# Attention without the turn of its result on TensorE, and values made for four key tiles at a time in place of two

## What is computed

```python
mod = (_silu(L0_c) @ L0_wmod).reshape(L0_c.shape[0], 6, 1, -1)
sa, ca, ga, sb, cb, gb = ...
h = _layernorm(x, axis=-1) * (1 + ca) + sa
x = x + ga * _L0_attn_ref(h, ...)        # q, k of 128 = 64 rope + 64 nope, latent of 32
h = _layernorm(x, axis=-1) * (1 + cb) + sb
x = x + gb * _L0_ffn_ref(h, ...)         # top 6 of 32 experts, plus the shared one

# inside _L0_attn_ref
scores = jnp.einsum('bhsd,bhtd->bhst', query, key) * scale
attn = jax.nn.softmax(scores.astype(jnp.float32), axis=-1)
out = jnp.einsum('bhst,bhtd->bhsd', attn, v)
return out.transpose(0, 2, 1, 3).reshape(B, S, H * VD) @ o_w.T
```

## Time and profile before

| | us |
|---|---|
| median of 3 runs | 2083.45 |
| range | 2078.28 to 2084.25 |
| the profiled execution | 2077.61 |
| its span, first to last instruction | 2075.7 |

### The profile page before, as it was taken

One profiled execution on the slowest core, in us unless ns is written; L12 is line 12 of the kernel. 1 busy time (PEld: TensorE's weight loads), 2 busy tenths in 40 slices (PEclk: granted clock), 3 DMA queues, 4 the chain that ended last, 5 costly groups with the idle time before them and its releaser, 6 DMA issues. The chain is left out here.

```text
span 2075.7 us, 44742 instructions
## 1 busy us (share of the span) xinstructions
PE 1918.5 (92%) x14050; PEld 1015.4 (49%) x14050; DVE 1354.4 (65%) x2858; ACT 1389.4 (67%) x1924; POOL 1347.8 (65%) x804
## 2 busy tenths in 40 slices
PE   8969999999999999999999999998855499999996
PEld 6623444444444444444444444443733367777765
DVE  5867777777777877777777778771532245555553
ACT  5617888888888888888888888887520135555543
POOL 2327888888888888888888888888256313333330
PEclk9969999999999999999999999999977699999998
DMA  6179970000000000000000000000123429999988
GB/s 235 46 311 406 407 274 0 0 0 0 0 0 0 0 0 0 0 0 0 0 0 0 0 0 0 0 1 3 55 81 123 140 94 338 343 347 346 337 277 288
DMA packets 87873, 231.12 MB, mean 111 GB/s; under 512 B 12048, under 2 KB 45072, under 8 KB 87696
## 3 DMA queue, kind: packets, MB, share of 16 engines
q1 hardware_dynamic: 77072, 200.32, 27.0%
q0 software_dynamic: 10752, 30.16, 3.8%
HBM read 126.33 MB, written 104.10 MB: 111 GB/s over the span
## 5 line engine op out<-in xcount | busy, mean ns | idle before, releaser
L813 POOL TENSOR_TENSOR prob_lo<-prob,prob_hi 128x1024 f16<-128x1024 f32 x512 | 1085.1, 2141 | 246.8 <-ACT prob_hi L836 246.8
L885 DVE TENSOR_REDUCE maxes<-ring 128x1 f32<-128x512 f32 x1024 | 645.0, 683 | 195.4 <-PE ring L987 187.6
L834 ACT ACTIVATE prob<-p_s,prob_scale 128x1024 f32<-128x1024 f32 x512 | 570.3, 1114 | 262.1 <-PE p_s L1021 260.6
L836 ACT ACTIVATE prob_hi<-p_s,prob_scale 128x1024 f16<-128x1024 f32 x512 | 570.2, 1114 | 0.0
L987 PE MATMUL ring<-kr_hi,qr_hi 64*128 64x512 f16 x1024 | 379.6, 385 | 13.6 <-DVE qc_hi L872 7.4
L987 PE MATMUL ring<-kc_pair,qc_hi 64*128 64x512 f16 x1024 | 375.5, 384 | 0.0
L1289 POOL DMA_INDIRECT ranked_out<-y,dest x128 | 122.7, 959 | 268.6 <-DVE y L1591 265.4
L1021 PE MATMUL p_s<-qr_lo,kr_hi 64*128 64x512 f16 x1024 | 293.0, 377 | 0.0
L1021 PE MATMUL p_s<-qr_hi,kr_lo 64*128 64x512 f16 x1024 | 283.2, 377 | 0.0
L1021 PE MATMUL p_s<-qr_hi,kr_hi 64*128 64x512 f16 x1024 | 250.3, 382 | 1.6 <-ACT prob_hi L836 1.5
L1021 PE MATMUL p_s<-qc_lo,kc_one 33*128 33x512 f16 x1024 | 248.1, 379 | 0.0
(11 more groups left out here) (253 smaller groups left out, 2665.9 us busy)
## 6 DMA issues: line engine op xcount, KB each, us to landing
w<-in_experts SPq DMA_DIRECT2D x128, 608.0 KB
expert_rows<-zeros SPq DMA_DIRECT2D x129, 544.0 KB, 7.7
rows<-expert_rows SPq DMA_DIRECT2D x128, 136.0 KB
got<-ranked_out SPq DMA_DIRECT2D x16, 768.0 KB, 10.4
wqb<-in_wqb SPq DMA_DIRECT2D x8, 768.0 KB, 5.0
cbar<-in_woT SPq DMA_DIRECT2D x1, 2048.0 KB, 16.3
ranked_out<-y,dest POOLq DMA_INDIRECT x128
out<-x SPq DMA_DIRECT2D x16, 128.0 KB, 3.6
```

Of the source, the lines that this page charges most:

```text
L813: gp.tensor_tensor(prob_lo[s % NB][:, :], prob[s % 2][:, :], prob_hi[s % NB][:, :], ALU.subtract).then_inc(lo_ready, 1)
L834: act.activation(prob[s % 2][:, :], p_s[s % 2][:, :], ACT.Exp, bias=prob_scale[:, :], scale=SCALE / W_SCALE)
L836: act.activation(prob_hi[s % NB][:, :], p_s[s % 2][:, :], ACT.Exp, bias=prob_scale[:, :], scale=SCALE / W_SCALE).then_inc(p_ready, 1)
L885: v.tensor_reduce(maxes[:, at:at + 1], bank[:, :], AX.X, ALU.max).then_inc(ring_used, 1)
```

## The change

Three things change.

- **No turn.** `turn` is gone from attention, and `turn_att` with its copies from `mixture`. `copy_out` writes one of two `att_t`. SyncE sends the two rows of sums to DRAM (`send_sums`) and fetches them back as 128 partitions of 8 (`fetch_sums`); VectorE inverts them (`invert`, at the start of group 1); SyncE sends the inverses to DRAM and spreads them over 32 partitions in each half (`send_recips`, `spread_recips`); VectorE multiplies `att_t` in place (`scale`, at the start of the last group); and SyncE stores the result in `cbar`, which now holds channels on partitions (`store_heads`). The last half-head's share of this is done at the head of `mixture`, where the projection of the second 1024 tokens waits for it.
- **`BATCH` = 4.** `plan` has four groups. Group `g` scores tiles `4g + 2` to `4g + 5` and then weighs tiles `4g` to `4g + 3`. The 32 maxima stand in groups 0 to 2 (10, 12 and 10), rope after the scores of group 2, rest after those of group 3, rows in group 3.
- **SyncE's order.** The blocks of `slots_dram` are cleared five at a time in the first 26 half-heads, each five between `spread_recips` and `store_heads`.

One wait is merged as well: the load of `wkz` counts on `ld_ov`.

```diff
-STEPS_V = 2 * 9
+STEPS_V = 2 * 8
...
-BATCH = 2
+BATCH = 4
+MOVES = 96
...
+def send_sums(sp, k, scaling, done):
+    att_t, recip_wide, sums, sums_dram, recips_dram = scaling
+    for c in range(2):
+        sp.dma_start(sums_dram[k:k + 1, c * QC:(c + 1) * QC],
+                     att_t[k % 2][c * CP + C:c * CP + C + 1, :]).then_inc(done, 16)
+def fetch_sums(sp, k, scaling, done):
+    sp.dma_start(sums[:, :], sums_dram[k:k + 1, :].rearrange("o (p j) -> (o p) j", p=P)).then_inc(done, 16)
+def send_recips(sp, k, scaling, done):
+    sp.dma_start(recips_dram[k:k + 1, :].rearrange("o (p j) -> (o p) j", p=P), sums[:, :]).then_inc(done, 16)
+def spread_recips(sp, k, scaling, done):
+    for c in range(2):
+        sp.dma_start(recip_wide[k % 2][c * CP:c * CP + C, :],
+                     recips_dram[k:k + 1, c * QC:(c + 1) * QC].to_broadcast([C, QC])).then_inc(done, 16)
...
-        MAX_AT = (MORE, LESS, MORE, MORE, LESS, MORE, NONE, NONE)
+        MAX_AT = (((0, 4, 7, 11, 16), (2, 5, 9, 13, 18)), ((0, 4, 7, 10, 14, 17), (2, 5, 9, 12, 15, 19)),
+                  ((1, 6, 10, 14, 17), (3, 8, 12, 15, 19)), ((), ()))
...
+            for k in range(2 * H - 1):
+                sp.wait_ge(o_copied, k + 2)
+                send_sums(sp, k, scaling, moved)
+                sp.wait_ge(moved, MOVES * k + 32)
+                fetch_sums(sp, k, scaling, moved)
+                if k:
+                    sp.wait_ge(stored, 32 * k)
+                    sp.sem_inc(freed, 1)
+                sp.wait_ge(answered, 2 * k + 1)
+                send_recips(sp, k, scaling, moved)
+                sp.wait_ge(moved, MOVES * k + 64)
+                spread_recips(sp, k, scaling, moved)
+                clear(min(5 * k, BLANKS), min(5 * k + 5, BLANKS))
+                sp.wait_ge(answered, 2 * k + 2)
+                store_heads(sp, k, scaling, cbar, stored)
...
-            def copy_out(m):
+            def copy_out(m, half):
                 v.wait_ge(o_mm, 16 * m + 16 + NB)
-                v.tensor_copy(att_t[:, :], p_o[:, :]).then_inc(o_copied, 1)
+                v.wait_ge(freed, m + 1)
+                v.tensor_copy(att_t[half][:, :], p_o[:, :]).then_inc(o_copied, 1)
+            def invert(m):
+                v.wait_ge(moved, MOVES * m + 48)
+                v.reciprocal(sums[:, :], sums[:, :]).then_inc(answered, 1)
+            def scale(m, half):
+                v.wait_ge(moved, MOVES * m + MOVES)
+                v.wait_ge(o_copied, m + 2)
+                v.tensor_tensor(att_t[half][0:CP + C, :], att_t[half][0:CP + C, :], recip_wide[half][0:CP + C, :],
+                                ALU.mult).then_inc(answered, 1)
...
                 for g in range(len(MAX_AT)):
-                    for now in plan(g, first, more, after):
+                    if g == 1 and not first:
+                        invert(m - 1)
+                    if g == len(MAX_AT) - 1 and not first:
+                        scale(m - 1, 1 - half)
+                    for now in plan(g, more, after):
...
-            def turn(m, use, bank):
-                pe.wait_ge(o_copied, m + 2)
-                pe.wait_ge(ring_used, use + 1)
-                for b in range(4):
-                    last = pe.transpose(bank[:, b * P:(b + 1) * P], att_t[:, b * P:(b + 1) * P], ident[:, :])
...
             def project(t):
-                pe.wait_ge(ct_ready, t + 1)
+                if t == T // 2:
+                    pe.wait_ge(stored, 64 * H)
```

165 lines of the change are left out of this document (86 added, 79 removed).

## The result

The changed kernel takes **2210.84 us** (median of 4 runs, 2204.77 to 2218.78) against 2082.75 for the kernel before, run beside it (4 runs, 2078.28 to 2084.25). The ratio is 1.0621 with a 95% interval of 1.0579 to 1.0663: **slower by 6.2%**. The forecast was 2190, with 2155 to 2225 for its unknown terms. The profiled execution is the slowest of the four, 2218.78 us with a span of 2216.8; against the profiled execution of before it is 141 us longer.

The account below looks back on a forecast made before the run. TensorE was taken as the bound, busy 40.00 of 40 us. Half-heads rise from 40.4 to 44.3 us, 122 us together; less 9 in `mixture`, net +113 on 2077.6 gives 2190 us, range 2155 to 2225.

Parts of the forecast that it names:

- The sign and the mechanism: Attention: slower, as TensorE idles for ScalarE's exponentials before scores, some 5 us in a half-head; net +113 us.
- The group's period: Each four-tile group in attention: 4.59 + 0.31 + 2.71 = 7.61 us, plus 0.216 per counted pair, plus any projection of 1.32.
- A and D: First and fourth of four tiles scored in a row; D may start 4.59 us after the start of A's last pair.
- The second wait: Start of a half-head: the fourth maximum waits for VectorE's split, copy and first reduction; 0.9 us, all on the path.
- The turn's 0.58 us: TensorE's turn, removed from each half-head of attention: a gain of 0.58 us.
- `scale` costs nothing: VectorE's multiply between rope work and `rows`, about the copy's 0.69 us; the delayed row has over 2 us to spare.
- The sum: 29 half-heads 113 us, the first 4.5, the 31st 2.5, the last 2: 122 more; less `mixture`'s 9, net +113.
- `mixture`: After attention: gives back 9 us, 2 for the last turn and 7 for turning back 16 tiles.
- The covered wait: Attention: other work covers the exponentials, leaving only gains; 57 us less, 2021 us, chance 0.07.
- The clock: Attention: TensorE's pauses drop its clock to 1.2 GHz for a quarter of the path; some 185 us more, 2375, chance 0.05.
- The DMAs: `invert` comes 5 us late in the 26 half-heads that also clear; 130 us more, 2320, chance 0.04.
- The smaller loss: Exponentials overlap more or the second wait is hidden; a half-head loses 2 to 3 us, 2130 to 2155, chance 0.05.

Follow-up runs that it names:

- experiment 2: The kernel before with groups of four tiles, the turn kept at the start of the second group; 2223.7 us, 1.068 of before.
- experiment 3: The changed kernel with each tile's first exponential on 512 of its 1024 columns; 2136.67 us, 1.0265 of before.
- experiment 5: The changed kernel with the one unused bank place moved from behind the first maximum to behind the sixth; 2195.95 us, 1.0572 of before.
- experiment 1: The changed kernel with groups of two tiles again and the old places of the maxima, still without the turn; 2078.31 us, 0.9988 of before.
- Experiment 7: The changed kernel with only group 0's maxima moved, so that its first tile's five pairs stand alone; 2157.88 us, 1.0377 of before.
- experiment 11: Two-tile groups, no turn, unused bank behind the sixth maximum, `scale` ahead of the fifth group's reductions on 8 of 512 columns; 2055.52 us, 0.9904 of before.
- 8: The changed kernel with all 32 maxima spread by another table over the first three groups; 2134.45 us, 1.0276 of before.
- experiment 4: The kernel before with each tile's first exponential on 512 of its 1024 columns; 2072.61 us, 0.9949 of before.

## Why the prediction was right, and where its terms were off

**The sign and the mechanism** were right. The kernel is slower because four tiles in a row wait twice in a group for two tiles of exponentials; experiment 2 shows that the group alone makes the loss, and experiment 3 that ScalarE's durations set it.

**The group's period**, 7.61 us and 0.216 for each pair of A and D: groups 1, 2 and 3 were to be 10.6, 11.5 and 10.7, and are 10.67, 11.54 and 10.67. Group 0 without the second wait was to be 10.6; group 1, which has the same pairs, shows it.

**The second wait** was there and was the mis-sized term: 0.9 us for it gave 11.5 for group 0, and the mean is 11.99. I followed the fourth maximum, as in the kernel before, and did not ask which bank each maximum now uses. With the unused bank behind the first one it is the third that waits for the first reduction. Tile A's last pair starts 3.30 or 2.82 us into the group, where group 1 has 1.74 (983.98 to 985.72): the term measured 1.32 and not 0.9. With the unused bank elsewhere (experiment 5) group 0 is 11.57 on the mean, the number of the forecast, and the same delay is 0.88. That makes 0.44 of the 0.56 us by which the step of 44.86 missed 44.3. Unrounded, the forecast's terms give 44.35, which leaves 0.07.

Even the 0.9 has some luck in it. I took it as 2.4 - 1.5. The fourth maximum starts in experiment 5 at 2.62 on the mean, and what counts is its distance from A's last pair, 1.74, not from its own place; the two misses of 0.2 cancel.

**The turn's 0.58 us**, counted as a gain, is there in its own group (experiment 1: 5.13 to 4.55) and is taken back in group 0: in the changed kernel by the order of the banks (experiment 5), with two tiles by that order and by `scale` in VectorE's chain. So the sentence that `scale` costs nothing was wrong in general and right for this kernel only as to what it delays: in the changed kernel VectorE idles 2.29 us between its steps and the cast of `qc_hi`, so `scale` is hidden; with two tiles there is no such gap. I priced it by the copy's 0.69 us and did not ask what it reads. The copy reads PSUM, `scale` reads SBUF twice, like GpSimd's subtraction.

**The sum.** 29 steps were to cost 113 us and cost 128.8. The first half-head was to cost 4.5 and cost 8.9 (first copy at 201.69 and 210.56); experiments 2 and 5, also in groups of four, have it at 205.15 and 205.91, 3.5 and 4.2 later than before, so some 4 to 5 us of the 8.9 came with the lower clock at its start. Experiment 7 has that too, 210.60, at the same clock as after in the stretch shown below. The busy rows of the start, of after and then of experiment 5, show the clock granted at 0.59 and at 0.84:

```profile
150.00:160.00 10.00, 8.82 (x51) 3.10 (x48) 4.04 (x8) 4.24 (x4) 2.78 (x2) 0.59 0.01 2
```

```profile
150.00:160.00 10.00, 5.72 (x40) 2.21 (x40) 5.40 (x9) 4.24 (x4) 4.24 (x2) 0.84 0.01 2
```

The 31st cost 2.8 (2.5). The last one cost 4.5 (2), of which two stretches at the lower clock are a part:

```profile
1555.00:1590.00 35.00, 27.67 (x210) 10.47 (x210) 0.89 (x2) 27.91 (x27) 28.76 (x15) 0.90 0.03 8
```

```profile
1557.89 0.61 PE L1090 MATMUL p_s<-qr_hi,kr_hi 64*128 64x512 f16 x2 [0.76 <-ACT prob_hi L908]
...
1558.71 0.64 PE L1090 MATMUL p_s<-qr_hi,kr_lo 64*128 64x512 f16 x2
1559.14 0.64 PE L1090 MATMUL p_s<-qc_hi,kc_pair 64*128 64x512 f16 x2
```

Here pairs follow at 0.43 us, after a wait of 0.76 us for ScalarE. Together the terms missed by 28 us in the profiled execution (141 for 113), of which the half-heads of the steady part are 16; that execution is the slowest of four, so the median lies only 21 above the forecast.

**`mixture`** was to give back 9 us and gave 3.8 in this pair of executions. Over all traces, the time behind the last copy is 628.0, 635.4 and 635.3 us in the three kernels with the turn (mean 632.9) and 618.4 to 625.7 in the eleven without (mean 622.3): 10.6 us. Its first tiles follow each other at 2.35 us, where the timeline of before has 2.78; the difference is the 0.43 us of turning in the earlier trace rows:

```profile
1605.00 1.89 PE L1700 MATMUL bank<-wov,cbar 128*128 128x256 f32 x8
...
1607.35 1.89 PE L1700 MATMUL bank<-wov,cbar 128*128 128x256 f32 x8
```

**The rivals.** The covered wait (2021 us) is excluded; even the best table leaves 51.2 of the 83.3 us. The clock (2375) is excluded for the steady part, at 1.00 with six pauses in a half-head. It showed itself in the last half-head, which takes 40.13 us, and 38.29 in experiment 5: by an estimate from these two, some 2 us. The Trainium skill ("TensorE: Matmul & The Clock Gate", section "A second HAM failure mode: psum-queue depth-cycling") tells of a clock that swings when TensorE idles shortly between its groups; the steady stretch, at 1.00, does not agree with that, the last half-head, at 0.90 from 1555 to 1590, does. The DMAs (2320) are excluded by the reciprocal that waits for nothing and by experiment 11. The smaller loss (2130 to 2155) is about what experiments 7 and 8 make by moving the maxima, which this change did not do.

## What to carry to other kernels

When a consumer with two buffers is fed in longer bursts, don't compare busy shares; add up one buffer's chain, from the end of the first item's production to the release of its neighbour's buffer, and compare it with the producer's other work inside the burst. Work that can go anywhere belongs inside that gap: the same 32 maxima cost up to 2.5 us a half-head more in other places. When buffers go round in a ring, write down for each use which earlier one it has to wait for; one unused place moved is worth 0.44 us here. And a step that is moved to an engine with time to spare has still three prices: the chain that it lengthens there, the buffer order that it shifts, and what it shares with other engines' operands.

## What the runs showed of the hardware

A VectorE operation that reads two SBUF operands and a GpSimd one that does the same exclude each other for their whole length: `scale` first by 0.02 us, and the pair of subtractions takes 4.73 us in place of 4.22; GpSimd first by 0.10 us, and `scale` takes 2.58 us in place of 0.68, while the pair of subtractions takes 4.66. On 8 columns, 0.15 us, it holds up nothing. The Trainium skill states this rule ("SBUF — State Buffer", section "SBUF: two separate sides"): VectorE and GpSimd share a pair of ports, whoever starts first has it for the whole instruction. The rows agree. Weighed before, it would have told me that `scale` has a price beside its length; the rows put it at up to 1.9 us on VectorE and some 0.5 on GpSimd.

The same shows in every kernel here, in the chain of VectorE that decides the second wait. VectorE and GpSimd of after, a f32 step beside an idle GpSimd and then two steps of the split:

```profile
1007.42 0.69 DVE L935 TENSOR_TENSOR qr_raw<-qr_raw,rot 128x512 f32<-128x512 f32 x1
...
1010.47 1.62 DVE L941 CAST qr_hi<-qr_raw 128x512 f16<-128x512 f32 x1
...
1014.09 2.13 POOL L885 TENSOR_TENSOR prob_lo<-prob,prob_hi 128x1024 f16<-128x1024 f32 x1
...
1014.99 1.77 DVE L945 TENSOR_TENSOR qr_lo<-qr_raw,qr_hi 128x512 f16<-128x512 f32 x1
```

The step that writes `qr_lo` ends 0.54 us behind the subtraction; it takes 1.77 to 1.90 us in all kernels but experiment 3. The cast of `qr_hi`, with one SBUF operand, takes 0.64 us in experiment 4 and 2.07 in experiment 2. No run moves these steps away from GpSimd's, so what they cost a half-head is not shown.

TensorE kept its full clock in stretches where it stood still six times in 45 us, and lost it twice in the last half-head between 1555 and 1590 us, each time behind two pauses of 1.13 and 0.76 us by the brackets (at 1555.88 and 1557.89, and at 1576.17 and 1578.18). The same two pauses at 1566.79 and 1568.80 left it at 1.00. What tells these apart, the runs don't say.
